# A transformer block on one core: GpSimd's two weight subtractions placed behind the first normalising, table casts placed in front of it, first projection waiting by blocks

## Chip, cores and metric

The kernel runs on one core of one Trainium2 chip. The metric is device time in microseconds (us) of one execution, and the median of several runs. The profile is one execution recorded by the hardware profiler; its own time stands beside the median below.

The engines are TensorE (PE in the rows; PEld is its weight load), VectorE (DVE), ScalarE (ACT), GpSimd (POOL) and SyncE (SP, which issues nearly all DMAs here).

## The reference

`x` is [4, 512, 512] in f32 (batch, tokens, features). One pre-norm block:

```
x = x + attn(layernorm(x))        # 32 heads of 16, causal, ALiBi bias, softmax
x = x + ffn(layernorm(x))         # silu(h @ Wg.T) * (h @ Wu.T) @ Wd.T, inner size 1376

attn(h): q, k, v = split(h @ w_attn + b_attn)     # w_attn 512 x 1536
         scores = q k / 16 + slope * (j - i), -inf where j > i
         out = softmax(scores) v;  return out @ w_proj + b_proj
```

## The kernel before, in words

**Precision.** Products are made of f32 numbers split in two parts. A high part is a cast to a reduced f32 format (`fp32r`), a low part is the number less its high part. A product of a block is then three matmuls (high x high, high x low, low x high), numbered n = 0, 1, 2 in `project`. ScalarE makes the high parts (`wqkv_hi`, `fT_hi`), VectorE or GpSimd the low ones (`wqkv_lo`, `fT_lo`).

**Start of the kernel** (the part that the change touches), for the first batch element:
- SP loads the four token tiles of `x`, then three small tables of rows (`qx_raw`, `kx_raw`, `qm_raw`, for the ALiBi terms and maxima), then the Q and K columns of `w_attn` in four quarters `k` of 128 rows (128x1024 each), the bias, the V columns, `w_proj` and its bias. Then it waits for `rows_cast`, stores the cast tables to DRAM, and loads them broadcast into `k_st` and `q_st`.
- VectorE takes the statistics of x (`statistics`, `moments`, L169 and L174), GpSimd computes `rstd` from them (`inverse_deviation`, L190 and L192), VectorE normalises x in four instructions of 128x512 (`normalise`, L183).
- VectorE then casts the three tables (L860 to L862) and subtracts the low parts of weight quarters 2 and 3 (L865). GpSimd subtracts those of quarters 0 and 1 (L660), right behind `rstd`. ScalarE has cast the four high parts (L698).
- TensorE transposes the normalised tokens into four banks (`transpose_tokens`, L1075), ScalarE casts each (`transposed_hi`, L702), VectorE subtracts each (`transposed_lo`, L871).
- TensorE waits for all low parts and all four transposed blocks and runs the first projections Q(0,0), K(0,0), V(0,0), V(0,1), Q(0,1), K(0,1), each 12 matmuls of 128x512 (L1101, L1096 for V). In front of the V tiles it waits for V's low parts, which VectorE makes in one instruction (L974) behind `transposed_lo`.
- Each Q or K tile is then read by ScalarE (`first_part`, L708), by VectorE (`remainder` into `rest`, L878), by ScalarE (`second_part`, L714) and by GpSimd (`third_part`, L640, which frees `rest` for the next tile). SP stores the parts to `stack_dram` and loads them back in the order of the stacks (`q_st`, `k_st`). The first scores (`scores`, L1132) need a stack.

**Later.** 32 chunks of four heads: scores, row maxima on VectorE (L903, causal mask added there), shifted scores, exponentials on ScalarE (L737), masking on GpSimd (L646, L650), values weighed by TensorE. Projections of later batch elements lie between them. The feed-forward part follows in a second block (L1251, L1545). All engines run fixed instruction streams in the order of the program, joined by semaphores; each engine's wait blocks what stands behind it.

The semaphores of the change: `normed` (normalising done), `w_hi_done` (ScalarE's weight casts, counted), `w_split` (GpSimd's low parts), `w_split_v` (VectorE's, counted with the statistics' one in front), `dve_read` (banks that VectorE has read: for a transposed block also "its low part is there"), `rows_cast`.

Of the kernel before, what the change touches and what calls it, by code (L numbers as in the profile page):

```python
# [19 lines left out]
KT = D // P  # L20
# [82 lines left out]
def dve_reads(*tile):  # L103

    return sum(kind in BY_DVE for (kind, _, _), _ in SEQ[:TILE_AT[tile] + 1])
# [72 lines left out]
def normalise(dve, src, dst, mv, rstd, moments_ready, rstd_ready, count):  # L178

    dve.wait_ge(moments_ready, count)  # L180
    dve.wait_ge(rstd_ready, count)
    for t in range(TT):
        last = dve.tensor_scalar(dst[:, t, :], src[:, t, :], mv[:, t, 0:1], rstd[:, t:t + 1], ALU.subtract, ALU.mult)  # L183
    return last
# [54 lines left out]
def attention(nc, x_d, wqkv_d, bqkv_d, wproj_d, bproj_d, qx_d, kx_d, tokens_dram, bank, ident, minus_half, fT_hi, fT_lo,  # L239
# [16 lines left out]
    with ExitStack() as ctx:  # L256
# [17 lines left out]
        mv = sb("mv", [P, TT, 2])  # L274
        rstd = sb("rstd", [P, TT])
# [346 lines left out]
        def _(pool):  # L622
# [11 lines left out]
            def reciprocal_deviation(b):  # L634
                inverse_deviation(pool, mv, rstd, minus_half, moments_ready, var_ready, rstd_ready, b + 1)
# [19 lines left out]
                pool.tensor_tensor(xr(b, t), xr(b, t), bproj[:, :], ALU.add).then_inc(xr_biased, 1)  # L655

            reciprocal_deviation(0)
            for k in range(2):
                pool.wait_ge(w_hi_done, k + 1)
                pool.tensor_tensor(wqkv_lo[:, k, 0:2 * D], wqkv_raw[:, k, 0:2 * D], wqkv_hi[:, k, 0:2 * D].bitcast(F32),  # L660
                                   ALU.subtract).then_inc(w_split, 1)
# [31 lines left out]

        @block.scalar
        def _(act):
            for k in range(KT):
                act.wait_ge(wqk_in[k], 16)
                act.copy(wqkv_hi[:, k, 0:2 * D], wqkv_raw[:, k, 0:2 * D]).then_inc(w_hi_done, 1)  # L698

            def transposed_hi(b, k):  # L700
                act.wait_ge(tile_done, tiles_done("T", b, k))
                act.copy(fT_hi[:, k, :], bank[tile_bank("T", b, k)][:, :]).then_inc(act_read, 1)  # L702
# [73 lines left out]
                act.copy(gu_hi[:, f, :], gu[:, f % 2, :]).then_inc(gu_hi_done, 1)  # L776

            for k in range(KT):
                transposed_hi(0, k)
            act.wait_ge(wv_in, 16)  # L780
            act.copy(wqkv_hi[:, :, 2 * D:3 * D], wqkv_raw[:, :, 2 * D:3 * D]).then_inc(w_hi_done, 1)
# [55 lines left out]
        def _(dve):  # L837
# [17 lines left out]
                last = statistics(dve, xt, stats, t)  # L855
            first_step(last)
            moments(dve, stats, mv, moments_ready)
            normalise(dve, xt, xt, mv, rstd, moments_ready, rstd_ready, 1).then_inc(normed, 1)
            dve.wait_ge(rows_in, 48)
            dve.tensor_copy(qx_sb, qx_raw).then_inc(rows_cast, 1)  # L860
            dve.tensor_copy(kx_sb, kx_raw).then_inc(rows_cast, 1)
            dve.tensor_copy(qm_sb, qm_raw).then_inc(rows_cast, 1)  # L862
            for k in range(2, KT):
                dve.wait_ge(w_hi_done, k + 1)
                first_step(dve.tensor_tensor(wqkv_lo[:, k, 0:2 * D], wqkv_raw[:, k, 0:2 * D],  # L865
                                             wqkv_hi[:, k, 0:2 * D].bitcast(F32), ALU.subtract))
            assert first_steps[0] == qk_split_count()

            def transposed_lo(b, k):
                dve.wait_ge(act_read, act_reads("T", b, k))  # L870
# [97 lines left out]
                                  ALU.subtract).then_inc(gu_lo_done, 1)  # L968

            for k in range(KT):  # L970
                transposed_lo(0, k)
            dve.wait_ge(bias_in, 16)
            dve.wait_ge(w_hi_done, KT + 1)
            first_step(dve.tensor_tensor(wqkv_lo[:, :, 2 * D:3 * D], wqkv_raw[:, :, 2 * D:3 * D],  # L974
# [83 lines left out]
        def _(pe):  # L1058
# [19 lines left out]
            def project(kind, b, i, lo=0, hi=3 * KT):  # L1078

                out = free(kind, b, i) if lo == 0 else bank[tile_bank(kind, b, i)]  # L1080
                if lo == 0 and kind in "QKV":
                    pe.wait_ge(dve_read, dve_reads("T", b, KT - 1))
                if lo == 0 and (kind, b) == ("P", B - 1):
                    pe.wait_ge(s_maxed, 3 * HEADS)
                for p in range(lo, hi):
                    k, n = p // 3, p % 3
                    if kind == "P":
                        if n == 0:
                            pe.wait_ge(attn_split, (b * G + k) * HALVES + i * P // HS + 1)
                        at = slice(i * P, (i + 1) * P)  # L1090
                        a, w = ((aT_hi, wproj_hi), (aT_hi, wproj_lo), (aT_lo, wproj_hi))[n]
                        last = pe.matmul(out[:, :], a[:, k, at], w[:, k, :], start=(p == 0), stop=(p == 3 * KT - 1))
                    elif kind == "V":
                        at = slice(i * P, (i + 1) * P)
                        a, w = ((fT_hi, wqkv_hi), (fT_hi, wqkv_lo), (fT_lo, wqkv_hi))[n]
                        last = pe.matmul(out[:, :], a[:, k, at], w[:, k, 2 * D:3 * D], start=(p == 0),  # L1096
                                         stop=(p == 3 * KT - 1))
                    else:
                        at = "QK".index(kind) * D + i * P
                        w, a = ((wqkv_hi, fT_hi), (wqkv_hi, fT_lo), (wqkv_lo, fT_hi))[n]  # L1100
                        last = pe.matmul(out[:, :], w[:, k, at:at + P], a[:, k, :], start=(p == 0),  # L1101
                                         stop=(p == 3 * KT - 1))
                if hi == 3 * KT:
                    last.then_inc(tile_done, 1)
# [70 lines left out]

            for k in range(KT):
                transpose_tokens(0, k)
            pe.wait_ge(w_split, 2)
            pe.wait_ge(w_split_v, qk_split_count())
            project("Q", 0, 0)  # L1180
            project("K", 0, 0)
            pe.wait_ge(w_split_v, v_split_count())
# [54 lines left out]
def qk_split_count():  # L1237

    return 1 + KT - 2
# [365 lines left out]
```

## Time and profile before

| | |
|---|---|
| median of 3 runs | 870.93 us (870.82 to 875.95) |
| the profiled execution | 872.66 us, its span 871.0 us |
| granted clock of TensorE, mean | 0.983 |
| PE busy | 814.4 us (94%) |
| PEld busy | 562.1 us (65%) |
| DVE busy | 501.1 us (58%) |
| ACT busy | 356.9 us (41%) |
| POOL busy | 186.0 us (21%) |
| instructions | 13365 |

The span runs from the first to the last instruction, and all times in the rows count from its start. A busy share is an average over stages of different kinds: VectorE's 58% holds a long stretch of attention in which it is rarely idle, and a feed-forward stretch in which it mostly waits. A row of a timeline merges equal instructions that follow one another, so its second number is from the start of the first to the end of the last. An instruction's time holds also the time for which it stood still for a shared resource after its start.

### The profile page before, as it was taken

The page shows a single profiled execution, that of the slowest core. Times are in us where ns is not written, and L with a number is a line of the kernel's source. Part 1 is how long each engine was busy: PE and PEld are TensorE (multiplying, and loading weights), DVE is VectorE, ACT ScalarE, POOL GpSimd, SP SyncE. Part 2 cuts the span into 40 slices and gives each one's busy share as a digit, 9 for nine tenths or more (in the row PEclk, how much of TensorE's full clock was granted, in tenths as well). Part 3 has the DMA queues.
Part 4 walks back from the last instruction along what each step waited for, and adds up shares of the span by engine and source line. Part 5 has one row for each costly group of instructions (what it writes and reads, how often), then busy time and mean ns, then how long its engine had stood idle before and what let it go on. Part 6 is the DMA issues. An engine that isn't in the chain of part 4 may idle for free. (4 is left out here: it accounts for less than half of the span.)

```text
span 871.0 us, 13365 instructions
## 1 busy us (share of the span) xinstructions
PE 814.4 (94%) x4576; PEld 562.1 (65%) x4576; DVE 501.1 (58%) x1539; ACT 356.9 (41%) x693; POOL 186.0 (21%) x336
## 2 busy tenths in 40 slices
PE   1989899999999999999988989999999999999998
PEld 1745355556555565555633668887888788878886
DVE  6498877877988789887884444342222312232223
ACT  4336656665566655666556333231111211121111
POOL 5213333342433424334233300000000000000000
PEclk9999899999999999999988999999999999999999
DMA  8683645655565565665742337004000400030001
GB/s 273 173 261 110 177 139 196 196 158 187 193 211 186 155 190 188 207 195 154 240 146 82 117 123 263 13 1 146 0 1 1 145 0 0 0 131 13 0 0 48
DMA packets 70563, 109.31 MB, mean 126 GB/s; under 512 B 13395, under 2 KB 38662, under 8 KB 70505
## 3 DMA queue, kind: packets, MB, share of 16 engines
q1 hardware_dynamic: 68457, 108.32, 38.7%
q8 instruction: 30, 0.49, 0.3%
q10 hardware_dynamic: 2048, 0.27, 0.2%
q14 instruction: 28, 0.23, 0.1%
HBM read 65.97 MB, written 42.32 MB: 124 GB/s over the span
## 5 line engine op out<-in xcount | busy, mean ns | idle before, releaser
L903 DVE CUSTOM_DVE_ANT_0 bank<-bank,mask_qk 128x512 f32<-128x512 f32 (+3 forms) x512 | 240.1, 513 | 53.9 <-PE bank L1132 51.5
L737 ACT ACTIVATE pt<-bank 128x512 f32<-128x512 f32 (+1 forms) x384 | 194.0, 529 | 136.3 <-PE bank L1154 123.6
L1154 PE MATMUL bank<-q_st,k_st 116*128 116x512 bf16 (+3 forms) x512 | 134.4, 306 | 13.9 <-ACT pt L737 12.1
L1473 DVE TENSOR_TENSOR gu<-bank,silu 128x512 f32<-128x512 f32 x40 | 27.7, 692 | 199.5 <-issue 120.0
L1132 PE MATMUL bank<-k_st,q_st 97*128 97x512 bf16 (+3 forms) x512 | 131.5, 307 | 9.2 <-DVE mx L903 4.2
L1251 PE MATMUL bank<-fT_hi,wgu_hi 128*128 128x512 f32 x224 | 88.0, 393 | 4.1 <-DVE wgu_lo L1443 4.1
L1132 PEld LDWEIGHTS bank<-k_st,q_st 97*128 97x128 bf16 x512 | 41.0, 98 | 77.6 <-issue 36.6
L1251 PE MATMUL bank<-fT_lo,wgu_hi 128*128 128x512 f32 x224 | 87.6, 391 | 0.0
L1251 PE MATMUL bank<-fT_hi,wgu_lo 128*128 128x512 f32 x224 | 87.6, 391 | 0.0
L1406 ACT ACTIVATE silu<-bank 128x512 f32<-128x512 f32 x40 | 23.9, 598 | 147.6 <-PE bank L1251 147.6
L1171 PE MATMUL bank<-pt,v_nat 128*32 128x512 f32 (+3 forms) x1024 | 81.6, 463 | 2.8 <-POOL pt L646 2.1
L646 POOL TENSOR_SCALAR_AFFINE_SELECT pt<-pt 128x256 f32<-128x256 f32 x128 | 56.2, 439 | 128.2 <-ACT pt L737 128.2
L1154 PEld LDWEIGHTS bank<-q_st,k_st 116*128 116x128 bf16 x512 | 45.1, 99 | 47.2 <-ACT pt L737 25.1
L198 POOL TENSOR_SCALAR mv<-mv 128x4 f32<-128x4 f32 x4 | 0.9, 229 | 346.5 <-DVE mv L174 346.5
L1411 ACT CAST w_hi<-gu 128x512 fp32r<-128x512 f32 x40 | 24.9, 621 | 114.1 <-DVE gu L1473 114.1
L903 DVE DVE_READ_ACCUMULATOR2_ANT mx<- 128x1 f32 x512 | 71.6, 140 | 0.0
L650 POOL TENSOR_SCALAR_AFFINE_SELECT pt<-pt 128x256 f32<-128x256 f32 x128 | 53.3, 416 | 81.4 <-ACT pt L737 81.2
L1545 PE MATMUL bank<-wd_hi,w_hi 128*128 128x512 f32 x176 | 68.8, 391 | 0.0
L1545 PE MATMUL bank<-wd_hi,w_lo 128*128 128x512 f32 x176 | 68.5, 389 | 0.0
L1545 PE MATMUL bank<-wd_lo,w_hi 128*128 128x512 f32 x176 | 68.5, 389 | 0.0
L1171 PEld LDWEIGHTS bank<-pt,v_nat 128*32 128x32 f32 x1024 | 30.7, 115 | 46.1 <-issue 29.9
L1101 PE MATMUL bank<-fT_hi,w_hi 128*128 128x512 f32 x128 | 56.4, 441 | 2.8 <-DVE fT_lo L871 2.6
(106 smaller groups left out, 1394.6 us busy)
## 6 DMA issues: line engine op xcount, KB each, us to landing
stack_dram<-scratch SPq DMA_DIRECT2D x32, 384.0 KB, 3.1
q_st<-stack_dram SPq DMA_DIRECT2D x32, 384.0 KB
k_st<-stack_dram SPq DMA_DIRECT2D x32, 384.0 KB
stack_dram<-scratch SPq DMA_DIRECT2D x32, 256.0 KB, 3.2
pv_dram<-weighed SPq DMA_DIRECT2D x32, 256.0 KB, 4.5
weighed<-pv_dram SPq DMA_DIRECT2D x17, 256.0 KB
xt<-x SPq DMA_DIRECT2D x16, 256.0 KB, 3.9
stack_dram<-scratch SPq DMA_DIRECT2D x32, 128.0 KB, 3.9
```

The costliest lines, as they stand in the source:

```text
L646: pool.affine_select(out=blocks, in_=blocks, compare_op=ALU.is_ge, fill=0.0, base=0, pattern=[[0, 2], [1, P]], channel_multiplier=-1).then ...
L650: pool.affine_select(out=blocks, in_=blocks, compare_op=ALU.is_ge, fill=0.0, base=0, pattern=[[0, 2], [1, P]], channel_multiplier=-1).then ...
L737: act.activation(pt[:, h % PT_RING, COL0[k]:COL0[k] + WIDE[k]], bank[3 + (3 * h + k) % 2][:, 0:WIDE[k]], ACT.Exp, scale=1.0 / HD).then_inc ...
L903: last = dve.tensor_tensor_reduce(bank[k][:, at:at + n], bank[k][:, at:at + n], mask_qk[:, S - n:S], 1.0, NEG, ALU.add, ALU.max, mx[:, h % ...
L1101: last = pe.matmul(out[:, :], w[:, k, at:at + P], a[:, k, :], start=(p == 0), stop=(p == 3 * KT - 1))
L1132: last = pe.matmul(bank[k][:, at:at + n], q_st[0:K_MAX, s, h % 4, t * P:(t + 1) * P], k_st[0:K_MAX, s, h % 4, 0:n], start=True, stop=True)
L1154: last = pe.matmul(bank[3 + u % 2][:, at:at + n], k_st[0:K_EXP, s, h % 4, t * P:(t + 1) * P], q_st[0:K_EXP, s, h % 4, t * P:S], start=True ...
L1171: last = pe.matmul(bank[6][32 * j:32 * j + 32, t * P:S], v_all[:, v:v + 2 * HD], pt[:, (4 * c + j) % PT_RING, at:at + n], start=(t == 0), ...
L1251: last = pe.matmul(out[:, :], a, c, start=(start and i == 0), stop=(stop and i == len(passes) - 1))
L1411: act.copy(gu_hi[:, f % GU, :], gu[:, f % 2, :]).then_inc(gu_hi_done, 1)
L1473: dve.tensor_tensor(gu[:, f % 2, :], bank[5 + 2 * (f % 2)][:, :], silu[:, f % 2, :], ALU.mult).then_inc(gu_done, 1)
L1545: last = pe.matmul(bank[t][:, :], a[:, f % GU, cols], w[:, f, :], start=(f == 0 and i == 0), stop=(f == FT - 1 and i == 2))
```

## The change

Four edits, all in the start of the kernel. The matrix products, their operands and their order within a tile are the same.

1. GpSimd waits for `normed` before its two weight subtractions.
2. VectorE casts the three tables in front of `normalise`.
3. The low parts of weight quarters 2 and 3 move on VectorE from in front of all `transposed_lo` to in front of `transposed_lo(0, 0)` and `transposed_lo(0, 2)`; on ScalarE the high part of quarter 3 moves from in front of the transposed blocks to between the second and the third.
4. TensorE's two waits in front of the first projections go; Q(0,0) alone waits block by block inside `project`.

```diff
             reciprocal_deviation(0)
+            pool.wait_ge(normed, 1)
             for k in range(2):
                 pool.wait_ge(w_hi_done, k + 1)
...
-            for k in range(KT):
+            def first_weights_hi(k):
                 act.wait_ge(wqk_in[k], 16)
                 act.copy(wqkv_hi[:, k, 0:2 * D], wqkv_raw[:, k, 0:2 * D]).then_inc(w_hi_done, 1)
+
+            for k in range(KT - 1):
+                first_weights_hi(k)
...
             for k in range(KT):
+                if k == 2:
+                    first_weights_hi(KT - 1)
                 transposed_hi(0, k)
...
             moments(dve, stats, mv, moments_ready)
-            normalise(dve, xt, xt, mv, rstd, moments_ready, rstd_ready, 1).then_inc(normed, 1)
             dve.wait_ge(rows_in, 48)
             dve.tensor_copy(qx_sb, qx_raw).then_inc(rows_cast, 1)
             dve.tensor_copy(kx_sb, kx_raw).then_inc(rows_cast, 1)
             dve.tensor_copy(qm_sb, qm_raw).then_inc(rows_cast, 1)
-            for k in range(2, KT):
+            normalise(dve, xt, xt, mv, rstd, moments_ready, rstd_ready, 1).then_inc(normed, 1)
+
+            def first_weights_lo(k):
                 dve.wait_ge(w_hi_done, k + 1)
...
             for k in range(KT):
+                if k % 2 == 0:
+                    first_weights_lo(2 + k // 2)
                 transposed_lo(0, k)
...
-                if lo == 0 and kind in "QKV":
+                first = (kind, b, i) == ("Q", 0, 0)
+                if lo == 0 and kind in "QKV" and not first:
                     pe.wait_ge(dve_read, dve_reads("T", b, KT - 1))
...
+                        if first and n == 0:
+                            pe.wait_ge(dve_read, dve_reads("T", b, k))
+                        if first and n == 2 and k < 2:
+                            pe.wait_ge(w_split, k + 1)
+                        if first and n == 2 and k >= 2:
+                            pe.wait_ge(w_split_v, k)
...
             for k in range(KT):
                 transpose_tokens(0, k)
-            pe.wait_ge(w_split, 2)
-            pe.wait_ge(w_split_v, qk_split_count())
             project("Q", 0, 0)
             project("K", 0, 0)
```

## Rows read from the trace of the kernel before

**Rows 1.** Windows: engines' busy us (x instructions), PEclk, DMA share, GB/s
```profile
60.00:200.00 140.00, 130.43 (x889) 74.01 (x889) 113.77 (x424) 85.46 (x177) 51.79 (x101) 0.98 0.56 172
```

**Rows 2.** Waits, 7 to 60 us: total, times, longest
```profile
PE bank L1101 <- DVE fT_lo L871: 2.6, 1, 2.6
```

**Rows 3.** Timeline of TensorE: start, us, what, [idle before <-releaser]
```profile
15.67 3.56 PE L1075 MATMUL bank<-ident,xt 128*128 128x128 f32 x16 [15.67 <-DVE xt L183]
21.82 0.47 PE L1101 MATMUL bank<-fT_hi,w_hi 128*128 128x512 f32 x1 [2.59 <-DVE fT_lo L871]
...
28.97 0.39 PE L1096 MATMUL bank<-w_hi,fT_hi 128*128 128x512 f32 x1
...
39.62 0.39 PE L1101 MATMUL bank<-fT_hi,w_lo 128*128 128x512 f32 x1
40.69 0.38 PE L1132 MATMUL bank<-k_st,q_st 97*128 97x512 bf16 x1 [0.67 <-DMA q_st<-slopes_dram]
```

**Rows 4.** Windows (PEclk behind POOL), and the page's row of 40 slices
```profile
23.00:24.00 1.00, 1.00 (x4) 0.71 (x4) 1.00 (x1) 0.00 (x0) 0.00 (x0) 0.50 1.05 136
...
PEclk9999899999999999999988999999999999999999
```

**Rows 5.** Timeline of VectorE, fine, the four normalising instructions
```profile
9.54 0.55 DVE L183 TENSOR_SCALAR xt<-xt,mv,rstd 128x512 f32<-128x512 f32 x1 [1.56 <-POOL rstd L192]
...
10.00 2.58 DVE L183 TENSOR_SCALAR xt<-xt,mv,rstd 128x512 f32<-128x512 f32 x1
...
12.50 3.03 DVE L183 TENSOR_SCALAR xt<-xt,mv,rstd 128x512 f32<-128x512 f32 x2
```

**Rows 6.** Timeline of GpSimd at the start
```profile
8.38 1.04 POOL L192 TENSOR_TENSOR rstd<-mv,minus_half 128x4 f32<-128x4 f32 x1
9.75 5.03 POOL L660 TENSOR_TENSOR w_lo<-pt,w_hi 128x1024 fp32r<-128x1024 f32 x2 [0.34 <-ACT w_hi L698]
...
9.75 2.54 POOL L660 TENSOR_TENSOR w_lo<-pt,w_hi 128x1024 fp32r<-128x1024 f32 x1 [0.34 <-ACT w_hi L698]
```

**Rows 7.** VectorE's L933, all 32, and one place on both timelines
```profile
L933 DVE SCALAR_TENSOR_TENSOR aT_lo<-weighed,bias_qkv,aT_hi x32: 389/584/1159, 121.6 to 499.7; 128x256 fp32r<-128x256 f32 x32
...
125.80 1.15 DVE L933 SCALAR_TENSOR_TENSOR aT_lo<-weighed,bias_qkv,aT_hi 128x256 fp32r<-128x256 f32 x1
...
125.51 1.16 POOL L640 TENSOR_TENSOR scratch<-scratch 128x512 bf16<-128x512 f32 x1 [2.67 <-ACT scratch L714]
```

**Rows 8.** Timeline of ScalarE at the start
```profile
8.63 1.04 ACT L698 CAST w_hi<-pt 128x1024 fp32r<-128x1024 f32 x1 [6.55 <-DMA pt<-w_qkv]
...
13.32 1.04 ACT L698 CAST w_hi<-pt 128x1024 fp32r<-128x1024 f32 x1 [0.43 <-DMA pt<-w_qkv]
16.80 0.59 ACT L702 CAST fT_hi<-bank 128x512 fp32r<-128x512 f32 x1 [2.43 <-PE bank L1075]
...
19.75 1.90 ACT L781 CAST w_hi<-pt 128x2048 fp32r<-128x2048 f32 x1
```

**Rows 9.** Timeline of VectorE, 15 to 31 us
```profile
15.45 0.41 DVE L860 CAST q_st<-pt 96x512 bf16<-96x512 f32 x1
...
16.69 2.46 DVE L865 TENSOR_TENSOR w_lo<-pt,w_hi 128x1024 fp32r<-128x1024 f32 x2
19.19 2.48 DVE L871 TENSOR_TENSOR fT_lo<-bank,fT_hi 128x512 fp32r<-128x512 f32 x4
21.75 2.29 DVE L974 TENSOR_TENSOR w_lo<-pt,w_hi 128x2048 fp32r<-128x2048 f32 x1
27.30 0.75 DVE L878 SCALAR_TENSOR_TENSOR scratch<-bank,bias_qkv,scratch 128x512 f32<-128x512 f32 x1 [3.25 <-ACT scratch L708]
30.05 0.75 DVE L878 SCALAR_TENSOR_TENSOR scratch<-bank,bias_qkv,scratch 128x512 f32<-128x512 f32 x1 [2.00 <-POOL scratch L640]
```

**Rows 10.** Issue of V's weights on SyncE; KB and us to landing
```profile
6.28 4.05 SPq L467 DMA_DIRECT2D pt<-w_qkv  x1
...
pt<-w_qkv SPq DMA_DIRECT2D x1, 1024.0 KB, 10.4
```

More of the change, by code:

```diff
@@ L866, in _ @@
                                              wqkv_hi[:, k, 0:2 * D].bitcast(F32), ALU.subtract))
-            assert first_steps[0] == qk_split_count()
             def transposed_lo(b, k):
@@ L970, in _ @@
             for k in range(KT):
+                if k % 2 == 0:
+                    first_weights_lo(2 + k // 2)
                 transposed_lo(0, k)
+            assert first_steps[0] == qk_split_count()
             dve.wait_ge(bias_in, 16)
```

## The prediction

> **What bounds the kernel now.** I read the windows of the long stages first, then the waits, then each engine's timeline of the start. Between 60 and 200 us VectorE is busy for 113.8 of 140 us and TensorE for 130.4 [rows 1], and every load, store and wait there is placed relative to the work before it. So nothing in the change speeds this part up; it can only start earlier. Then the waits up to 60 us: TensorE waits 2.6 us for VectorE's `fT_lo` before the first projection [rows 2]. Then TensorE's own timeline [rows 3]: transposes from 15.67, first projection at 21.82, V's first matmul at 28.97, the last of the 72 matmuls at 39.62, the first scores at 40.69, behind 0.67 us of waiting for a load of the stacks. From 28.97 to 39.62 there are 47 steps, so 0.2266 us per matmul. [...] What counts is therefore the time of the first scores, 40.69, and two chains meet there: TensorE's 72 matmuls (done 40.0), and first projection, parts, stores, stacks (40.69).
>
> Last the start itself. The first normalising instruction takes 0.55 us, and the four begin 0.46 us apart when nothing is in the way (9.54 and 10.00); but the second takes 2.58 us, and the last two together 3.03 [rows 5]. Over the same time GpSimd runs its two weight parts, 9.75 to 14.78 [rows 6]. VectorE's second instruction ends at 12.58, just behind GpSimd's first (12.29): the two engines take turns, and who comes second stands still. So a GpSimd part holds VectorE for about 2.24 us (10.05 to 12.29), a VectorE step of normalising holds GpSimd for about 0.3.
>
> **The change, part by part.**
>
> (a) Normalising without GpSimd. Four steps from 9.54 would end at 9.54 + 3 x 0.46 + 0.55 = 11.47 rather than 15.53: 4.06 us. TensorE's transposes follow 0.14 us behind.
>
> (b) The three table casts in front. They cost 0.41 us each and start 0.45 apart [rows 9], 1.35 in all, and stand where VectorE was idle for 1.56 us waiting for GpSimd's `rstd` [rows 5]. Their loads are queued between x and the first weights, which ScalarE reads from 8.63 [rows 8], so they have landed by about then and perhaps well before; I take "before". But GpSimd computes `rstd` in the same gap, the longer of its two operations from 8.38 to 9.42 [rows 6], and if those take turns with the casts as the parts did with the normalising, up to two casts (0.8) are put in front of GpSimd or behind it. Bounds: 0 and 0.9 us. Between the ends, at nothing held and at the turn of a whole instruction, no row decides (GpSimd's work here is on 128x4, beside [rows 5] on 128x1024); I take the middle, 0.45. Normalising then ends at 11.9, transposes start at 12.05, 3.6 us earlier than 15.67. If nothing in the gap hid the casts they would cost 1.35. [...]
>
> (c) SP's stores of the tables wait on the casts, behind the load of `bproj`; they now leave when that issue is done, and so do the two broadcasts behind them. TensorE needs those only at the first scores. They meet the loads of V's weights and of `wproj`; V's land 10.4 us after the issue at 6.28, at 16.7 [rows 10], while ScalarE comes to them at 16.7 at the earliest. Cost 0; if they were late by 1 us, still 0, as VectorE needs V's low part only by 22.6.
>
> (d) ScalarE: before, its first transposed cast starts 1.13 us behind TensorE's first transpose and lasts 0.59 [rows 3, 8], transposed banks coming 0.85 apart. Now: T0 13.2 to 13.8, T1 14.0 to 14.6, fourth weight cast 14.6 to 15.65 (1.05, as in rows 8), T2 to 16.25, T3 to 16.8, V's high parts to 18.7. Before, it had cast its third weight quarter by 13.3, where it began the fourth [rows 8]; so the one is there by then as before, and the other's data is there at 14.6.
>
> (e) GpSimd and VectorE share the low parts, and both read two SBUF operands. Does VectorE's subtraction wait too? One place in the trace says yes: at 125.80 a VectorE instruction with two SBUF operands takes 1.15 us beside GpSimd's 1.16 us from 125.51, where the median of its 32 is 0.584 and the shortest 0.389 [rows 7]. So in turns: GpSimd k0 12.05 to 14.3; VectorE k2, ready by 13.3, 14.3 to 15.5 (1.2, as in rows 9); GpSimd k1 15.5 to 17.7; VectorE T0 and T1 low parts 15.55 to 16.8 (0.62 apart, from a bank, so not held); VectorE k3 held until 17.7, then to 18.9; T2 and T3 low parts to 20.25. Before, T3's ended at 21.7. The turns cost up to 1.0 us (k2) and 0.9 us (k3); without any they would be 0, with GpSimd taking both its turns in a row 2.4 more than none.
>
> (f) First projection by blocks. Its waits stand behind nothing but itself. k0 can start at 16.35, k1's third matmul at 17.85, k2 at 19.75, k3 at 20.4. So nine of its twelve matmuls run in time in which TensorE was idle, and 63 of 72 are left at 20.4. Last matmul: 20.4 + 62 x 0.2266 = 34.45, done at 34.9, if the clock stays; with the same 1.7 us lost as before, 36.6. I take the loss as kept, since TensorE is as idle between 13 and 20 as it was before the drop of before; bounds 0 and, if the level stays low longer, see the rivals.
>
> (g) The other chain. The first projection is done at 21.3 (fast clock) or 21.9, ScalarE's first part at 22.1 to 22.7. What is late next is V's low part on VectorE, 2.29 us [rows 9], from 20.3 to 22.6, in front of the first `rest`: so that starts at 22.65, where it was 27.30. The second one, of K, came 2.75 later (30.05), as GpSimd's third part frees `rest`: now 25.4. With the slow clock K's projection is done at about 25.3 and ScalarE's part of it at 26.0: `rest` at 26.1, 3.95 earlier than 30.05. From there to the first scores everything is relative: 40.69 - 3.95 = 36.75, or 36.05 at full clock.
>
> **Sum.** TensorE's chain 36.6, the stacks' 36.75: the first scores start 3.9 us earlier, at full clock 4.6. I take 4.0, all of it reaching the end. The profiled execution takes 872.66 (span 871.0 and 1.66 around it), so it would be 868.7; it stands 1.7 above the median of the runs, 870.93, which goes to **866.9**.
>
> [...]
>
> **The rivals.**
> 1. *GpSimd isn't held by turns, and takes k0 and k1 in a row* (12.05 to 16.5). VectorE: k2 to 17.7, T0, T1 to 19.0, k3 to 20.2, T2, T3 to 21.55, V's low part to 23.85; `rest` of Q 23.9, 3.4 us earlier, TensorE's chain from 21.7: 3.0 with the clock loss. Against: the turn at 12.29 [rows 5]. Time 867.9. Chance 0.12.
> 2. *No contention of the low parts*, or no clock loss, or both. VectorE ends T3 at 18.1 and V's low part, behind ScalarE's 18.7, at 21.0: both chains 5 to 6.3 us earlier. Against: [rows 7] and [rows 4]. Time 864.6 to 866. Chance 0.17.
> 3. *Slower: the clock stays low.* From 20.4 on each matmul at the lower level costs up to twice 0.2266. Its place is the run of projections up to the first scores. The end at full clock is 34.9, before was 40.0: from 5.1 / 0.2266 = 23 such matmuls on, 10 us of low level, the change loses. All 63 low: done at 49.2, first scores 8.5 later than before, time 879.4. [...] Against: before, the level came back as soon as the matmuls ran on, 3 to 4 us later. Chance 0.03.
> 4. *The gain is given back later*: nothing is left at the end, 870 to 871.5, since later low levels of the clock fall otherwise. The page's clock row has three slices at 8 tenths, one around 100 us and two around 457 [rows 4], and a low level costs up to the 1.7 us of the first one where TensorE is the bound. Chance 0.10.
> 5. *It doesn't do what it says*: the table casts wait for their loads or for GpSimd's `rstd`, and normalising begins some 1.35 late or more. Then all is 0.9 later than in my sum: 867.8. Chance 0.08.
>
> **How the numbers follow.** Forecast 866.9, chance 0.50, own range 865.9 to 867.9 (casts' cost 0 to 0.9; loss of clock kept). Range for 8 in 10: from rival 2's 864.3 to 870.2, with one half of rival 4 and rival 3 left out. A measurement of this kernel tells 1% (8.7 us) from no change at best. Faster by over 1% would want 862.2, more than the 6.3 us that the freest case gives: 0.03. Slower by over 1% is a share of rival 3 and of what I don't see: 0.03. Within 1%: 0.94.
>
> **What would show it.** Four normalising instructions of 0.55 us ending near 11.9; transposes from 12.05; GpSimd's first part from there, with VectorE's k2 recorded at about 2.5 us, for the wait is in it; first scores at 36.8 where they were 40.69; a low clock level once between 18 and 28. Wrong would be: casts of over 1 us, `rstd` later than 10.3, two GpSimd parts back to back with VectorE's behind both, or the first scores earlier with the end where it was.

## The result, and the profile after

Over 22 runs each, the median went from 874.03 to 869.3 us. The ratio taken over the runs is 0.9955, with a 95% interval of 0.9939 to 0.9971: 3.9 us faster, 2.5 to 5.3 (the two medians alone would give 0.9946). Set against the median before, 870.93, that is 867.0, where 866.9 was forecast. The same kernel was measured twice more, on other occasions, with a dozen runs each: 0.9980 (0.9953 to 1.0007) and 0.9977 (0.9954 to 1.0000). All three intervals share 0.9954 to 0.9971, but the last two lie nearer 2 us; weighed by their intervals the three give some 3 us, an estimate. Three executions that took 936, 1348 and 2050 us are left out of the ratios. What follows rests on the traces of the start, which repeat within 0.6 us in the changed kernel; the times only bound it.

VectorE's timeline of the changed kernel, to be laid beside [rows 5] and [rows 9]:

```profile
8.07 0.38 DVE L174 BATCH_NORM_AGGREGATE mv<-stats 128x2 f32<-128x6 f32 x4
8.42 0.42 DVE L865 CAST q_st<-pt 96x512 bf16<-96x512 f32 x1
...
9.32 0.41 DVE L867 CAST q_st<-pt 15x512 bf16<-15x512 f32 x1
10.32 1.92 DVE L183 TENSOR_SCALAR xt<-xt,mv,rstd 128x512 f32<-128x512 f32 x4 [0.58 <-POOL rstd L192]
13.27 2.48 DVE L872 TENSOR_TENSOR w_lo<-pt,w_hi 128x1024 fp32r<-128x1024 f32 x1 [1.04 <-ACT w_hi L699]
15.79 1.29 DVE L877 TENSOR_TENSOR fT_lo<-bank,fT_hi 128x512 fp32r<-128x512 f32 x2
17.00 2.07 DVE L872 TENSOR_TENSOR w_lo<-pt,w_hi 128x1024 fp32r<-128x1024 f32 x1
19.10 1.29 DVE L877 TENSOR_TENSOR fT_lo<-bank,fT_hi 128x512 fp32r<-128x512 f32 x2
20.31 2.28 DVE L983 TENSOR_TENSOR w_lo<-pt,w_hi 128x2048 fp32r<-128x2048 f32 x1
22.71 0.75 DVE L884 SCALAR_TENSOR_TENSOR scratch<-bank,bias_qkv,scratch 128x512 f32<-128x512 f32 x1
25.47 0.75 DVE L884 SCALAR_TENSOR_TENSOR scratch<-bank,bias_qkv,scratch 128x512 f32<-128x512 f32 x1 [2.00 <-POOL scratch L640]
...
38.33 0.70 DVE L909 CUSTOM_DVE_ANT_0 bank<-bank,mask_qk 128x512 f32<-128x512 f32 x1 [1.28 <-PE bank L1148]
```

The four normalising instructions take 1.92 us together instead of 6.0. The two weight subtractions take 2.48 and 2.07 us where they took 1.2 each [rows 9]: the wait beside GpSimd has moved from the one to the other, and is smaller there. GpSimd at the same time (beside [rows 6]):

```profile
8.54 0.39 POOL L190 TENSOR_SCALAR mv<-mv 128x4 f32<-128x4 f32 x1 [2.19 <-DVE mv L174]
9.01 1.18 POOL L192 TENSOR_TENSOR rstd<-mv,minus_half 128x4 f32<-128x4 f32 x1
12.31 5.67 POOL L661 TENSOR_TENSOR w_lo<-pt,w_hi 128x1024 fp32r<-128x1024 f32 x2 [2.12 <-DVE xt L183]
```

TensorE (beside [rows 3]):

```profile
12.38 3.65 PE L1084 MATMUL bank<-ident,xt 128*128 128x128 f32 x16 [12.38 <-DVE xt L183]
16.54 0.80 PE L1117 MATMUL bank<-fT_hi,w_hi 128*128 128x512 f32 x1 [0.51 <-DVE fT_lo L877]
17.13 0.63 PE L1117 MATMUL bank<-fT_lo,w_hi 128*128 128x512 f32 x1
...
18.84 0.63 PE L1117 MATMUL bank<-fT_hi,w_lo 128*128 128x512 f32 x1
19.85 0.79 PE L1117 MATMUL bank<-fT_hi,w_hi 128*128 128x512 f32 x1 [0.38 <-DVE fT_lo L877]
...
20.71 0.40 PE L1117 MATMUL bank<-fT_hi,w_lo 128*128 128x512 f32 x1
...
35.01 0.39 PE L1117 MATMUL bank<-fT_hi,w_lo 128*128 128x512 f32 x1
37.59 0.58 PE L1148 MATMUL bank<-k_st,q_st 97*128 97x512 bf16 x1 [2.19 <-DMA q_st<-slopes_dram]
```

The first projection begins at 16.54 instead of 21.82. Its first matmuls stand 0.43 us apart, where the usual step is 0.2266, as in the stretch of the kernel before that stood at 0.50 [rows 4]; but k2, and k3 behind it, had to wait for VectorE until 19.85 anyway, and from 20.71 on the steps are 0.23 again. The last of the 72 matmuls starts at 35.01 instead of 39.62, 4.6 us earlier. The first scores start only 3.1 us earlier, at 37.59 instead of 40.69, after 2.19 us of waiting for the stacks (0.67 before). So a new wait ate 1.5 us of the gain. SyncE's queue shows where it is from; changed kernel first, then the kernel before (the rows are the last store of the tables, the first broadcast, the six stores of parts, the loads of the first stacks of q and of k):

```profile
14.96 0.33 SPq L475 DMA_DIRECT2D q_rows_dram<-q_st  x1
21.53 0.29 SPq L477 DMA_DIRECT2D k_st<-k_rows_dram  x1
...
25.39 4.31 SPq L491 DMA_DIRECT2D stack_dram<-scratch  x6
31.46 0.34 SPq L499 DMA_DIRECT2D q_st<-stack_dram  x1
33.47 0.33 SPq L499 DMA_DIRECT2D k_st<-stack_dram  x1
```

```profile
17.57 0.34 SPq L475 DMA_DIRECT2D q_rows_dram<-q_st  x1
20.65 0.29 SPq L477 DMA_DIRECT2D k_st<-k_rows_dram  x1
...
29.98 4.31 SPq L491 DMA_DIRECT2D stack_dram<-scratch  x6
34.33 0.67 SPq L499 DMA_DIRECT2D q_st<-stack_dram  x1
36.54 0.33 SPq L499 DMA_DIRECT2D k_st<-stack_dram  x1
```

The tables' stores leave 2.6 us earlier, but SyncE waits 6.2 us for them to land (2.7 before), so the broadcasts are issued 0.9 us *later* (at 20.73 and 20.59, as before, in the two other executions of the changed kernel); and the stores of parts now come 3.5 us behind them, not 9. The last of these stores is issued by 29.70. The loads behind it need Q's parts, then K's, to have landed: 1.76 and 3.77 us later, where before it was 0.04 and 2.25. The DMA engines show the overlap (windows, columns as in [rows 1]; the last two are DMA share and GB/s). Just before the first store of parts they stood still in the kernel before; in the changed kernel they are busy, and move little, as the stores begin:

```profile
29.00:30.00 1.00, 1.00 (x6) 0.84 (x5) 0.00 (x0) 0.69 (x1) 0.95 (x1) 1.00 0.00 0
```

```profile
25.00:26.00 1.00, 1.00 (x6) 0.80 (x6) 0.53 (x1) 0.25 (x1) 0.36 (x1) 1.00 0.83 48
```

Two corrections are needed before kernels are compared. The loads of x reach VectorE at different times from one execution to the next: its aggregates (L174), which nothing of the change touches, began between 6.79 and 8.40 us. So the start is measured from there to the first maxima (L903 in the kernel before), which can't begin before the first scores. (In some kernels, before among them, VectorE was still at a `rest` when the first scores came, which adds up to 0.6 us. From the aggregates to the first scores it is 33.09 us before and 29.52, 29.11 and 29.11 in the changed kernel: 3.6 to 4.0 shorter, where the table gives 3.7 to 4.3.) The column "`rest` to scores" runs from the start of K's `rest` to the first scores, the stretch in which the stacks are stored and loaded. And one execution's end says little, for a reason shown further below.

| kernel | aggregates at | first maxima at | between | `rest` to scores | ratio to before (95% interval) |
|---|---|---|---|---|---|
| before | 7.60 | 41.58 | 33.98 | 10.64 | |
| changed | 8.07 | 38.33 | 30.26 | 12.12 | 0.9955 (0.9939 to 0.9971) |
| changed, second time (`e9_changed_again`) | 8.01 | 37.65 | 29.64 | 11.87 | 0.9980 (0.9953 to 1.0007) |
| changed, third time (`e12_changed_third`) | 7.84 | 37.49 | 29.65 | 11.68 | 0.9977 (0.9954 to 1.0000) |
| edit 1 alone (`e1`) | 6.96 | 41.33 | 34.37 | 10.45 | 1.0015 (0.9994 to 1.0036) |
| edits 2 to 4 (`e2`) | 8.40 | 39.40 | 31.00 | 10.72 | 0.9963 (0.9937 to 0.9989) |
| edit 4 alone (`e3`) | 8.26 | 39.04 | 30.78 | 10.89 | 0.9989 (0.9967 to 1.0011) |
| edits 1 to 3 (`e10`) | 6.79 | 38.84 | 32.05 | 10.72 | 0.9980 (0.9960 to 1.0001) |
| edits 1, 3, 4 (`e8`) | 7.78 | 39.68 | 31.90 | 10.73 | 0.9965 (0.9938 to 0.9993) |
| changed, tables stored first (`e4`) | 7.83 | 37.15 | 29.32 | 10.92 | 0.9952 (0.9926 to 0.9979) |
| changed, low parts on VectorE (`e5`) | 8.21 | 37.23 | 29.02 | 12.23 | 0.9977 (0.9955 to 1.0000) |
| both (`e6`) | 7.85 | 35.99 | 28.14 | 11.27 | 0.9962 (0.9939 to 0.9986) |
| changed, broadcasts late (`e7`) | 8.08 | 43.51 | 35.43 | 17.31 | 1.0031 (1.0005 to 1.0057) |
| both, broadcasts cut (`e11`) | 7.28 | 37.02 | 29.74 | 10.63 | 0.9986 (0.9966 to 1.0007) |

The kernels were run in three groups, each with its own runs of the kernel before: e1 to e4; e5, e6, e8, e9; e7, e10, e11, e12.

### The profile page after: what moved, and what is told of

Its sections match the earlier page's. It is cut to its first block and busy times, and to the rows that moved or that the text cites. A ratio compares the mean times of both kernels' runs of the same rounds, so it can differ in the third digit from the quotient of the medians.

```text
span 871.1 us, 13365 instructions
## 1 busy us (share of the span) xinstructions
PE 816.1 (94%) x4576; PEld 563.4 (65%) x4576; DVE 500.6 (57%) x1539; ACT 357.6 (41%) x693; POOL 187.4 (22%) x336
## 5 line engine op out<-in xcount | busy, mean ns | idle before, releaser
L1487 DVE TENSOR_TENSOR gu<-bank,silu 128x512 f32<-128x512 f32 x40 | 27.7, 692 | 200.6 <-issue 121.1
```

Source lines behind the costliest of these rows:

```text
L1487: dve.tensor_tensor(gu[:, f % 2, :], bank[5 + 2 * (f % 2)][:, :], silu[:, f % 2, :], ALU.mult).then_inc(gu_done, 1)
```

## Experiments

**Edit 1 alone.**

```diff
             reciprocal_deviation(0)
+            pool.wait_ge(normed, 1)
             for k in range(2):
```

> The kernel before with the first edit alone: GpSimd waits for the normalising, nothing else moved. Theory A (the two engines take turns at a shared way to SBUF): normalising takes 1.9 us instead of 6.0 and ends at 11.5, transposes from 11.6; but the three casts and the two subtractions of VectorE now take turns with GpSimd's parts, so the four low parts of the transposed blocks end at about 21.9, as before, and the time is within 1 us of before. Theory B (nothing is shared, the normalising was slow for a reason of its own): its four instructions still take 6 us, transposes at 15.7. Theory C (an earlier normalising is worth its 4 us whatever stands behind it): first projection 4 us earlier, time 4 us lower.

VectorE's timeline:

```profile
8.91 1.92 DVE L183 TENSOR_SCALAR xt<-xt,mv,rstd 128x512 f32<-128x512 f32 x4 [1.57 <-POOL rstd L192]
10.74 0.42 DVE L861 CAST q_st<-pt 96x512 bf16<-96x512 f32 x1
11.19 2.49 DVE L862 CAST q_st<-pt 20x512 bf16<-20x512 f32 x1
13.71 2.46 DVE L863 CAST q_st<-pt 15x512 bf16<-15x512 f32 x1
16.09 2.47 DVE L866 TENSOR_TENSOR w_lo<-pt,w_hi 128x1024 fp32r<-128x1024 f32 x2
```

The four normalising instructions take 1.92 us: theory B falls. The gain is gone right behind them: the second and third cast take 2.49 and 2.46 us beside GpSimd's two parts (4.99 us together from 10.90), where each took 0.41, and the last low part of a transposed block ends 14.1 us behind the aggregates, as before. Start 34.37 us, 0.4 more than before, time the same: theory A, and C falls. VectorE, waiting its turn, loses about 2.1 us here with casts that take 0.41.

**The change without edit 1.** The same line, taken out of the changed kernel.

> The changed kernel without its first edit: GpSimd starts its parts as soon as it may. Theory A: normalising again takes about 6 us and ends at about 16, transposes follow; VectorE's two subtractions then take 1.2 us each instead of 2.5 and 2.1, so the last low part of a transposed block ends at about 21.5 where the changed kernel has 20.4: about 1 us slower than the changed kernel, still 2 to 3 us faster than before, since the waits by blocks remain. Theory B': the wait is what brings the gain, so without it the time is that of before.

```profile
10.56 5.97 DVE L183 TENSOR_SCALAR xt<-xt,mv,rstd 128x512 f32<-128x512 f32 x4 [0.57 <-POOL rstd L192]
16.46 1.21 DVE L871 TENSOR_TENSOR w_lo<-pt,w_hi 128x1024 fp32r<-128x1024 f32 x1
18.50 1.48 DVE L876 TENSOR_TENSOR fT_lo<-bank,fT_hi 128x512 fp32r<-128x512 f32 x2 [0.82 <-ACT fT_hi L705]
20.23 1.23 DVE L871 TENSOR_TENSOR w_lo<-pt,w_hi 128x1024 fp32r<-128x1024 f32 x1 [0.25 <-ACT w_hi L698]
```

Normalising takes 5.97 us again, and the two subtractions 1.21 and 1.23. So the order decides who stands, and for how long: VectorE stood still for 4.05 us here and for 4.1 in e1, but for 2.1 in the changed kernel, where part of GpSimd's work falls beside subtractions from a bank (1.29 us for two, with GpSimd beside them and without). The start is 31.00 us, 0.7 to 1.4 more than the changed kernel's and 3.0 less than before's: theory A. The last low part of a transposed block ends 2.0 us later behind the aggregates than in the changed kernel, where about 1 was expected, since VectorE also waits 0.82 and 0.25 us for ScalarE. About three quarters of the start's gain stay without the edit that the change begins with.

**Edit 4 alone** (`project` and the waits in front of it as changed, all else as before; the diff is the last two hunks of the change).

> The kernel before with the fourth edit alone: the first projection waits block by block. The low parts of the transposed blocks are ready from 19.9 to 21.7 as before, so nine of twelve matmuls run before 21.8 and the tile is done at about 22.7 instead of 26.4; V's low part on VectorE then holds the first rest until 24.1, 3.2 us earlier than 27.3; first scores 36.8 to 37.6 (40.7 before), time 2.5 to 3.5 us lower. If the first edit brings the gain, this one has at most 1 us.

TensorE's first projection and the first scores:

```profile
20.63 0.50 PE L1108 MATMUL bank<-fT_hi,w_hi 128*128 128x512 f32 x1 [0.61 <-DVE fT_lo L871]
...
38.51 0.38 PE L1139 MATMUL bank<-k_st,q_st 97*128 97x512 bf16 x1 [1.25 <-DMA q_st<-slopes_dram]
```

First `rest` at 24.87, 16.6 us behind the aggregates (19.7 before), start 30.78, 3.2 us shorter than before: as expected by the trace. The time is less clear: 0.9989, 1 us faster, and -2.9 to +1.0 by its interval, where 2.5 to 3.5 was expected. TensorE's 71 steps from 20.63 to the last of the 72 at 36.87 take 16.24 us, 0.229 each: there is no stretch at the lower clock in them. (Before, the first 24 matmuls took 7.15 us where 24 steps of 0.2266 are 5.44, at a clock of 0.50 from 23 to 24 us [rows 3, 4].) The pause in front is 0.61 us where it was 2.59 [rows 3]; whether that is why can't be said from this run, as will be seen below.

**The changed kernel without edit 4.**

> The changed kernel with the fourth edit undone: the first projection waits for all low parts, as before; edits 1 to 3 stay. The low parts end 12.3 us behind the aggregates (14.1 before), so the projection starts 12.4 behind (14.2 before): 1.7 us of the gain comes from the first three edits, the clock's drop falls on the projections again (1.7 us), and first maxima come 32 to 32.5 behind the aggregates (before 34.0, changed 29.6 to 30.3). If the blocks were worth little: 30.5.

Start 32.05, as expected: edits 1 to 3 together shorten it by 1.9 us, and edit 4 takes off another 1.8 to 2.4. With the 3.2 us of edit 4 alone that makes 5.1, more than the 3.7 to 4.3 of all four: the two parts overlap. The projection starts 12.5 us behind the aggregates, after 4.50 us of idle time, and its first matmuls are 0.43 apart (19.85, 20.28, 20.70).

**The changed kernel without edit 2**, that is, `normalise` again in front of the three casts.

> The changed kernel with the second edit undone: the three table casts stand behind the normalising, everything else as changed. Theory A: normalising starts 0.8 us earlier against the aggregates (GpSimd's rstd is not held by the casts), but the casts run beside GpSimd's parts; in turns, one of them stands 2.2 us, and the low parts end 1 to 3 us later than in the changed kernel; first maxima 31 to 32.5 behind the aggregates. If the place of the casts doesn't matter (rival), 30.3.

Normalising starts 1.95 us behind the aggregates (2.25 in the changed kernel, so the casts in front cost 0.3, where 0.8 was expected), and the start is 31.90 us, 1.6 to 2.3 longer. Two of the casts take 2.48 and 2.46 us, not one: the expected range was met, its mechanism was too mild.

**Low parts all on VectorE.**

```diff
-            pool.wait_ge(normed, 1)
-            for k in range(2):
-                pool.wait_ge(w_hi_done, k + 1)
-                pool.tensor_tensor(wqkv_lo[:, k, 0:2 * D], ...).then_inc(w_split, 1)
...
+            for k in range(2):          # VectorE, behind its normalising
+                dve.wait_ge(w_hi_done, k + 1)
+                dve.tensor_tensor(wqkv_lo[:, k, 0:2 * D], ...).then_inc(w_split, 1)
```

> The changed kernel with all four first low parts on VectorE, none on GpSimd. Theory A (VectorE's subtractions stand still beside GpSimd's): the two that took 2.5 and 2.1 us take 1.2 each, as the two new ones do, so four cost 4.8 where two cost 4.55 plus 1.0 idle in front: the low parts of the transposed blocks end 0.8 us earlier than in the changed kernel against the end of the statistics, and the first scores no earlier, as the stacks' loads are what is late there (theory D). Rival (GpSimd's share really is spared work): 2.4 us later, first scores 2 us later.

```profile
12.21 2.35 DVE L872 TENSOR_TENSOR w_lo<-pt,w_hi 128x1024 fp32r<-128x1024 f32 x2
14.48 1.22 DVE L867 TENSOR_TENSOR w_lo<-pt,w_hi 128x1024 fp32r<-128x1024 f32 x1
...
16.93 1.21 DVE L867 TENSOR_TENSOR w_lo<-pt,w_hi 128x1024 fp32r<-128x1024 f32 x1
```

Four subtractions cost 4.8 us (2.35 for two, 1.22, 1.21), where two had cost 4.55, with 1.04 of idle time in front. In this start GpSimd's help was worth less than nothing: the first `rest` comes 13.49 us behind the aggregates instead of 14.5 to 14.7. The part of the expectation that the start would be no shorter was wrong: it is 29.02, 0.6 to 1.2 less. Waiting for the stacks, TensorE is idle 2.52 us in front of the first scores.

**Tables stored first.**

```diff
+            sp.wait_ge(rows_cast, 3)
+            sp.dma_start(slopes_dram..., qx_sb)       # and the two others
             sp.dma_start(wproj_raw[:, :, :], ...).then_inc(wproj_in, 16)
             sp.dma_start(bproj[:, :], ...).then_inc(bproj_in, 16)
-            sp.wait_ge(rows_cast, 3)
-            sp.dma_start(slopes_dram..., qx_sb)       # and the two others
             sp.wait_ge(rows_stored, 48)
```

> The changed kernel, with SyncE storing the cast tables ahead of the loads of w_proj and its bias. Theory D (the stores and the broadcasts behind them collide with the parts' stores, since they queue behind w_proj): the table stores land at about 17.5 instead of 20.4, the broadcasts are issued there and not at 21.5, the six stores of parts land within 3 us again, the first scores start at about 36.0 instead of 37.6: 1.5 us faster than the changed kernel, 4 to 5.5 faster than before. Rival E (the stores of parts were late for another reason, such as the number of small packets): first scores stay at 37.6 and the time as it was.

SyncE's queue (broadcast, stores of parts, loads of q's and k's stack):

```profile
17.62 0.32 SPq L477 DMA_DIRECT2D k_st<-k_rows_dram  x1
...
25.57 4.31 SPq L491 DMA_DIRECT2D stack_dram<-scratch  x6
29.91 0.68 SPq L499 DMA_DIRECT2D q_st<-stack_dram  x1
32.30 0.33 SPq L499 DMA_DIRECT2D k_st<-stack_dram  x1
```

The broadcast is issued at 17.62, 3.9 us earlier. The last store of parts is issued by 29.88, q's load follows 0.03 us later and k's 2.42: the delays of before (0.04 and 2.25) are back. So theory D holds for the delay: broadcasts in flight hold up q's parts by 0.9 to 1.7 us and k's by 0.5 to 1.4 (the three executions of the changed kernel against e4). Three other runs agree. In e2, e8 and e10 the broadcasts leave at the same time as in the changed kernel (20.95 to 21.13), but the stores of parts come later, at 27.26 to 28.07, and there q's and k's loads follow the last store by 0.04 to 0.05 and 2.25 to 2.29 us. The start gains less than was expected, 29.32 us against 29.64 to 30.26, since in this execution the first projection ended 0.4 us later behind the aggregates (first `rest` at 15.05 instead of 14.64): the lower clock lasted into two more matmuls, behind the wait for VectorE (20.29, 20.71 and 21.12, 0.42 and 0.41 us apart, where the changed kernel has 0.27 and 0.24 from 20.44 on).

**Both.**

> Both: tables stored ahead of w_proj and all four low parts on VectorE. If both theories hold, the gains add: 1.0 to 1.5 us from the broadcasts and 0.5 to 0.8 from the low parts, first maxima 28.5 to 29.0 us behind the aggregates (changed 30.3, before 34.0), 1.5 to 2.3 us faster than the changed kernel. If the stacks' loads are the bound alone, it is as with the tables first: 29.3.

28.14 us: 1.2 less than with the tables alone, 0.9 less than with the low parts alone, 1.5 to 2.1 less than the changed kernel, 5.8 less than before, and 0.4 below the range that was expected. It is the best start. The delay is smaller here, not gone: q's load follows the last store by 0.73 us, k's by 2.76. Its time, 0.9962 in a group in which the changed kernel had 0.9980, is lower by 1.6 us of medians (868.92 against 870.56), but the intervals overlap, so that it beats the changed kernel is shown for the start alone.

**Broadcasts behind the stores of parts.** The block of the two broadcasts moved behind `store_parts("K", 0, 0)`.

> The changed kernel with the two broadcasts of table rows moved behind the six stores of Q's and K's first parts. Theory D (broadcast packets are slow and hold up the stores): with no broadcast in flight SyncE's last store is issued 4.3 us behind the first and the first stack load follows within 0.3 us, not 1.3 to 1.8 us; but the broadcasts now run beside the stack loads and take 6 to 7 us, so first scores 29 to 32 us behind the aggregates (changed 29.1 to 29.5). Rival E: the gap in front of the first stack load stays at 1.3 us or more.

The load of q's first stack is issued at 30.97 and k's at 32.08, 2.4 us behind the last store, near the 2.25 of before: the stores aren't held up now. (For q this run decides nothing: SyncE is at the broadcasts' issue until 30.93, 1.25 us behind the last store.) But the broadcasts come late themselves, TensorE waits 7.6 us, and the first scores start 34.69 us behind the aggregates, 2.7 over the upper end of what was expected; 1.0031 is the one ratio whose interval lies above 1. The first scores, which need the broadcasts and the first stack, start 13 us behind the issue of the broadcasts, where I had counted 6 to 7.

**Both, with the broadcasts cut in two** (slots 0 and 1, then slots 2 and 3 behind the loads of the first two stacks, with a semaphore of their own that TensorE waits for at the ninth head).

> Tables stored ahead of w_proj, all low parts on VectorE, and the broadcasts cut in two: the rows of stack slots 0 and 1 where they were, those of slots 2 and 3 behind the first stack loads. Theory D: half the broadcast ends 3 us sooner, before the first stores of parts (16 us behind the aggregates), the first stack load follows the stores within 0.5 us, first maxima 27.0 to 27.7 behind the aggregates (both together without the cut: 28.15). If the second half delays the third stack, TensorE waits before the ninth head and the gain is given back: the time is then that of both together.

The start is 29.74 us, not 27.0 to 27.7. The loads of the first stacks do follow the last store by 0.04 and 2.26 us, but the stores came 6.0 us behind the broadcasts, as in e10, where nothing was cut. In this execution the first projections were late already (V's low part starts 13.5 us behind the aggregates, 11.3 without the cut), which the cut can't have caused, as it comes later on the queue; and TensorE waited 2.0 us for stacks after 40 us. What the start had gained was then given back: against before and counted from the aggregates, VectorE is through the first chunk's maxima 4.2 us earlier and through the third's no earlier, where without the cut (e6) it is 5.8 us earlier at both. The load behind the second stores of parts goes out at 49.37 us (45.27 without the cut). So the second half's cost is seen in one trace; what it would be with a punctual start is left open, and the time, 0.9986, says only that it is no gain.

**The changed kernel again,** twice, for the comparison within the groups.

> The changed kernel itself, on the same chip as the next three. Theory A with D: the end of the statistics (VectorE's aggregates) varies by about 1 us with the loads of x, and behind it the first maxima come 30.3 us later, where before it was 34.0: 3 to 4 us faster than before, ratio 0.9955 give or take 0.0015, with SyncE's wait for the table stores at about 6 us again. If the 6 us wait and the late stacks were an accident of one execution (rival), the wait is below 4 us here.

> The changed kernel on the chip of the three others, to compare them: 29.6 to 30.3 us from the aggregates to the first maxima, ratio to before between 0.994 and 0.998.

SyncE's wait for the tables' stores was 5.7 and 6.0 us (6.2 the first time): no accident. The start was 29.6 us both times.

**Why one execution's end says little.** The profiled execution of the changed kernel took 872.76 us, that of before 872.66, though its first maxima came 3.3 us earlier; the third one's span was 864.1. The two executions of the same kernel in windows (columns as in [rows 1]), first the one that took 872.76, then the third:

```profile
85.00:95.00 10.00, 8.48 (x70) 3.93 (x69) 7.65 (x33) 5.83 (x13) 2.95 (x8) 1.00 0.43 133
95.00:112.00 17.00, 14.76 (x83) 6.42 (x83) 11.88 (x50) 8.89 (x19) 3.58 (x9) 0.80 0.52 157
```

```profile
85.00:95.00 10.00, 8.85 (x62) 3.42 (x61) 7.31 (x31) 4.99 (x12) 2.51 (x7) 0.83 0.41 130
95.00:112.00 17.00, 14.95 (x104) 8.23 (x103) 13.96 (x57) 10.95 (x25) 4.78 (x12) 1.00 0.58 171
```

Between 85 and 112 us one has 17 us at a mean clock of 0.80, the other 10 at 0.83: about 6.8 against 3.4 us at the lower level, which is 0.50 in both (103 to 109 us in the one, 89 to 92 in the other). VectorE did 19.5 us of work in one and 21.3 in the other. Such stretches lie at other places in each execution (e2 has one more, 0.57 from 57 to 61 us, e8 0.53 from 55 to 58, and there the start's gain shrank by 1 to 2 us on the way to 97 us). What becomes of the start's gain can be followed by the end of each chunk's maxima (where VectorE starts `mparts`), counted from the aggregates and set against the kernel before. The three executions of the changed kernel are ahead by 3.2, 4.3 and 4.3 us at the first chunk (48.9 us before), by 3.2, 4.5 and 4.3 at the fifth (96.6), and by 3.0, 4.2 and 6.8 at the seventh (122.1), behind these stretches. So the gain is carried for 50 us, within 0.2, and then changes where the clock changes. Runs of one kernel spread over 8 us; that the clock makes most of this spread is likely, not shown. A start that is 4 us shorter shows in many runs only.

## Why the prediction was right

It was right in the sum, 4.0 us against 3.9, and that is partly luck: K's `rest` came 1.1 to 1.3 us earlier than forecast and the way from there to the first scores was 1.0 to 1.5 us longer, and the two later measurements give about 2 us. That all of the start's gain reaches the end, as the sum had it, is open: the start, counted to the first scores, is 3.6 to 4.0 us shorter in all three traces, while the times gave 3.9, 1.7 and 2.0 us. The lower end of the range for 8 in 10, 864.3, should have been 864.6, rival 2's own.

The forecast's times count from the trace of before, with its aggregates at 7.60. The changed kernel's came at 8.07, so 0.47 is taken off its times below; its two other executions are treated alike. Step by step:

- **(a) Normalising alone**: 1.93 expected, 1.92 measured. e1 and e2 show the cause by removing and restoring it.
- **(b) Casts in the gap**: I took 0.45, between 0 and 0.9; it was 0.31, 0.22 and 0.32 (normalising 2.25, 2.16 and 2.26 us behind the aggregates, 1.94 before). GpSimd's two operations grew from 0.23 and 1.04 to 0.39 and 1.18 us. GpSimd's operation doesn't hold VectorE here: the third cast, at 9.32, took 0.41 us inside GpSimd's 9.01 to 10.19. Its large ones do: e1's casts took 2.49 and 2.46 us beside parts of 2.5.
- **(c) SyncE's stores at no cost: wrong.** This is the step that failed. I had the broadcasts leave earlier with the stores, and weighed only their meeting with the loads of V's weights and of `w_proj`. The tables' stores queue behind these 2 MB and land at 20.6 to 21.5 us, issued from 13.3 on or from 16.8 on; ahead of `w_proj` (e4) they land by 17.6. The broadcasts then meet the stores of parts, which are the ones that moved. Cost: 1.0 to 1.5 us between K's `rest` and the first scores (12.12, 11.87 and 11.68 us, before 10.64). e4 takes all but 0.3 of it away (10.92).
- **(d), (e) ScalarE and the low parts by turns**: VectorE's k2 was forecast to end at 15.5 and k3 at 18.9, and ended at 15.3 and 18.6; T3's low part at 20.25, was 19.9; V's at 22.6, was 22.1. e5 shows the price of the turns: without them four subtractions cost 4.8 us, where two cost 4.55.
- **(f) Blocks, and the clock: too dear.** The 1.7 us that I kept for the clock are what the first 24 matmuls took before, 7.15 us, less 24 steps of 0.2266 [rows 3]; that the changed kernel would pay them again was my estimate. The lower level came, by steps of 0.43 us from the first matmul at 16.54 and so sooner than the 18 to 28 that I had named, and it lay on matmuls that waited for VectorE anyway. 36.6 was forecast for the end of the projections and 34.9 measured, the value at full clock. The second execution of the same kernel shows the price, for it had no drop:

```profile
16.39 0.50 PE L1117 MATMUL bank<-fT_hi,w_hi 128*128 128x512 f32 x1 [0.60 <-DVE fT_lo L877]
16.72 0.39 PE L1117 MATMUL bank<-fT_lo,w_hi 128*128 128x512 f32 x1
```

Its first `rest` starts 14.48 us behind the aggregates, against 14.64 and 14.68 with the drop: 0.2 us. So the lower level came in two of the three executions of the changed kernel, and the price that I had put on it, 1.7 us, wasn't paid. What decides about the drop, told here by steps of 0.43 us, is open. Behind pauses in front of the first projection of 2.59 (before), 3.46 (e8), 4.50 (e10) and 6.61 us (e1) it came each time; behind short ones it came after 0.39 (e5), 0.50, 0.51 and 0.52 us (e4) and not, by steps of 0.23 to 0.24, after 0.41 (e6), 0.56 (e7), 0.60, 0.61 (e3) and 0.89 (e11).
- **(g) First `rest`**: forecast 22.65, measured 22.2; K's 26.1, measured 25.0, and 25.4 was its value for the full clock.
- **First scores**: forecast 36.75, measured 37.1, 36.7 and 36.7. My sum at full clock was 36.05; so (f) gave 0.7, VectorE's low parts, ready sooner, another 0.4 to 0.6, and (c) took 1.0 to 1.5.

Of the rivals, 1 (no turns) and the first half of 2 (no contention) are refuted by the 2.48 and 2.07 us and by e5. The second half of 2, no loss to the clock, came true, and (c) ate what it gave at the first scores. Of 3 the drop came without its price; 5 didn't occur. Rival 4, that the gain is given back later, isn't excluded in part: the two later measurements keep about half of it, with intervals that reach from nothing to all. What the prediction didn't say is how the start's gain divides: edit 4 alone shortens it by 3.2 us, edits 1 to 3 by 1.9, edit 1 by nothing, all four by 3.7 to 4.3, in one execution of each but the last.

## What to carry to other kernels

When two engines take turns, as VectorE and GpSimd did here, moving one of them can move the wait to what the other does next: VectorE's 4.1 us at the normalising became 4.1 at two casts in e1, and 2.1 at two subtractions in the changed kernel. Look what stands there, and put work there that the traces show unheld (a bank's subtractions, 1.29 us for two beside GpSimd and without) rather than small copies, which were held for 2.1 us each (2.49 and 2.46 for 0.41). When a stage moves forward, list the transfers in flight at its new time; those issued behind a wait for landings need not move with it: here the stores of parts came 4.6 us earlier, and the broadcasts, behind SyncE's 6.2 us of waiting, 0.9 later. And look at a gate that waits for everything before making its producers faster: split into blocks it gave 3.2 us of start here, the faster producers behind it 1.9, though the times (0.9989 and 0.9980) don't tell the two apart.

## What the runs showed of the hardware that I had not expected

- GpSimd's subtractions of 128x1024 slow VectorE's casts of 15 and 20 partitions in e1, 2.46 and 2.49 us for what takes 0.41, as much as its normalising on 128: 2.58 for 0.55 [rows 5].
- GpSimd's operation on 128x4 doesn't hold VectorE's cast of 0.41 us, but takes 0.14 us longer itself (1.18 in the changed kernel for 1.04 before).
- The granted clock's records showed 1.00 between 16 and 20 us in the changed kernel while its matmuls were 0.43 us apart, and 1.00 as well in its second execution, where they were 0.23 apart; so there the step between matmuls tells the two apart and the records don't.
- Broadcast loads of 320 and 240 KB keep the DMA engines busy (0.83 from 25 to 26 us) at 48 GB/s, and q's first load, which waits for stores beside them, is issued 1.76 us behind the last store, where before it was 0.04.
- Two executions of one kernel differ by 3.4 us of lower clock in one place and by 7 us of span.
